# Neighbour lists of a graph network: two tiles sorted in turn, the second sort cut to 32, shorter records

## The reference

```python
def _graph_conv(x, src, dst, W, b, R, num_nodes):
    agg = jax.ops.segment_max(x[src], dst, num_segments=num_nodes)
    agg = jnp.where(jnp.isneginf(agg), 0.0, agg)
    return agg @ W + b + x @ R
...
edge_index = jnp.stack([src, dst])
h = jnp.maximum(_layernorm(x, axis=-1), 0.0)
x = x + _L0_gnn_ref(h, edge_index, ...)
h = jnp.maximum(_layernorm(x, axis=-1), 0.0)
x = x + _L1_gnn_ref(h, edge_index, ...)
```

## Time and profile before

| | us |
|---|---|
| median of three runs | 6179.05 |
| lowest, highest | 6169.71, 6181.23 |
| the profiled execution | 6172.75 |
| its span, first to last instruction | 6170.6 |

### The profile page before, as it was taken

How to read it: one execution, slowest core, us unless ns; L and a number is a source line. 1 busy time by engine, 2 the same in 40 slices (tenths; PEclk the granted TensorE clock), 3 DMA queues, 4 the chain that set the end, 5 groups by cost and what they waited for, 6 DMA issues and landing times. The chain is left out here.

```text
span 6170.6 us, 53373 instructions
## 1 busy us (share of the span) xinstructions
PE 4170.1 (68%) x16801; PEld 1892.4 (31%) x16801; DVE 4641.7 (75%) x7595; ACT 962.0 (16%) x2799; POOL 3126.4 (51%) x3104
## 2 busy tenths in 40 slices
PE   6660001499988881888888677766787587757675
PEld 5430001123322220443444333333333243323332
DVE  7799993477766662999999786767787687768775
ACT  0010000100000001767777300001000100010000
POOL 0300003567777776300000277776777677767776
PEclk9999996799999995999999898888999899979887
DMA  0249921444444441655555443334433443344332
GB/s 16 53 160 420 421 84 42 122 134 128 139 119 120 124 113 41 185 169 162 166 168 176 132 127 105 115 110 114 123 120 115 111 125 115 116 106 122 113 110 70
DMA packets 357598, 819.67 MB, mean 133 GB/s; under 512 B 96893, under 2 KB 211283, under 8 KB 357012
## 3 DMA queue, kind: packets, MB, share of 16 engines
q1 hardware_dynamic: 208468, 564.72, 27.2%
q0 software_dynamic: 99456, 172.85, 11.4%
q10 hardware_dynamic: 49392, 78.70, 4.6%
HBM read 580.78 MB, written 235.22 MB: 132 GB/s over the span
## 5 line engine op out<-in xcount | busy, mean ns | idle before, releaser
L2041 PE MATMUL c_wide<-c_choice,c_parts 128*128 128x512 fp8e4 (+1 forms) x8232 | 1762.8, 371 | 669.0 <-DVE c_even L2129 282.8
L1916 POOL DMA_INDIRECT c_ring<-table,near x1720 | 1652.7, 961 | 524.2 <-issue 524.2
L2041 PEld LDWEIGHTS c_wide<-c_choice,c_parts 128*128 128x128 bf16 x8232 | 809.7, 102 | 1597.6 <-issue 333.9
L2129 DVE TENSOR_TENSOR c_even<-c_even,c_wide 128x896 f32<-128x896 f32 x672 | 726.0, 1080 | 62.9 <-PE c_wide L2041 57.8
L1619 ACT ACTIVATE b_weighed<-b_onehot,mask_r 128x128 f32<-128x128 bf16 x2401 | 719.7, 387 | 228.5 <-DVE b_onehot L1681 228.5
L2129 DVE TENSOR_TENSOR c_odd<-c_odd,c_wide 128x896 f32<-128x896 f32 x644 | 695.8, 1080 | 78.7 <-PE c_wide L2041 74.0
L1658 PE MATMUL b_agg<-b_mass,b_h_row 128*128 128x512 f32 (+1 forms) x1372 | 600.3, 569 | 224.1 <-DVE b_mass L1689 121.3
L2144 DVE TENSOR_REDUCE c_staged<-c_ring 128x128 f32<-128x1024 f32 (+15 forms) x196 | 400.2, 2042 | 419.3 <-DMA c_ring<-table,near 419.1
L1309 PE MATMUL a_logits<-a_hidden,a_w_col 128*49 128x512 f32 (+1 forms) x1372 | 601.6, 562 | 132.6 <-DVE a_hidden L1364 126.2
L1364 DVE TENSOR_TENSOR a_hidden<-a_wide,a_minus_bt 128x896 f32<-128x896 f32 x343 | 373.1, 1088 | 310.9 <-PE a_wide L1290 310.8
L1175 POOL DMA_INDIRECT masks<-a_value,a_cell x430 | 470.2, 1093 | 131.1 <-issue 130.2
(11 more groups left out here) (276 smaller groups left out, 4094.7 us busy)
## 6 DMA issues: line engine op xcount, KB each, us to landing
masks<-n_zeros SPq DMA_DIRECT2D x196, 784.0 KB, 13.7
b_mass<-masks SPq DMA_DIRECT2D x343, 448.0 KB, 3.5
c_choice<-chosen SPq DMA_DIRECT2D x196, 784.0 KB
a_pick_row<-picks ACTq DMA_DIRECT2D x343, 224.0 KB, 3.9
chosen<-a_choice SPq DMA_DIRECT2D x49, 784.0 KB, 4.4
c_ring<-table,near POOLq DMA_INDIRECT x1720
c_source<-table SPq DMA_DIRECT2D x28, 448.0 KB, 6.3
a_ring<-table_a,near POOLq DMA_INDIRECT x430, 3.2
```

Of the source, the lines that this page charges most:

```text
L1916: pool.indirect_dma_start(ring[:, at + j, :], None, table1[layer % 2], bass.IndirectOffsetOnAxis(near[:, u, j:j + 1], 0)).then_inc(landed[ ...
L2041: last = pe.matmul(wide[q][:, lo_c:hi_c], parts[:, s, part, :], choice[e][:, s % CHUNK, lo_c:hi_c], start=(part == 0), stop=(part == 2))
L2129: dve.tensor_tensor(side[:, :], side[:, :], found, ALU.max).then_inc(taken, 1)
```

## The change

The constant `NEAR` is 32. The second sort takes four rounds in place of eight, over the same 64 columns; `record` keeps 32 near neighbours in place of 64, so it has 85 integers, 340 bytes, and `near` and the copies into `laid` are 32 columns shorter. Two tiles are sorted in turn: each step is issued for tile t and tile t+1 after each other, from buffers of their own, and waits for all but the last instruction; the eight instructions of the split become eight such steps. The 49th tile goes alone. The general way is now taken also when a node has more than 32 marked neighbours: `most` becomes the larger of the largest degree and the largest `load` + 32, and is known only behind the sorts, so its spreading by PE and the computation of `slow` and `fast` move there.

```diff
+
+NEAR = 32
...
-RECORD = INFO + BLOCK + TILES
+RECORD = INFO + NEAR + TILES
...
+NEAR_ROUNDS = NEAR // 8
...
-        near = sb("near", [P, TILES, BLOCK], I32)
+        near = sb("near", [P, TILES, NEAR], I32)
...
-            digit_i = sb("n_digit_i", [P, BLOCK], I32)
...
+            work = [[[sb(f"n_work{e}{m}{p}", [P, BLOCK]) for p in range(2)] for m in range(2)] for e in range(2)]
+            top = [[sb(f"n_top{e}{m}", [P, BLOCK]) for m in range(2)] for e in range(2)]
...
             @block.tensor
             def _(pe):
-                pe.wait_ge(most_made, 1)
-                pe.matmul(all_most[:, :], bc(most[:, :], [P, P]), ident[:, :], start=True,
-                          stop=True).then_inc(most_spread, 1)
                 pe.wait_ge(w_loaded, 3 * 16)
                 pe.wait_ge(h_made, 1)
...
                         last.then_inc(ab_made[q], 1)
+                pe.wait_ge(most_made, 1)
+                pe.matmul(all_most[:, :], bc(most[:, :], [P, P]), ident[:, :], start=True,
+                          stop=True).then_inc(most_spread, 1)
 
...
                 own.did(dve.tensor_tensor(degree[:, :], degree[:, :], real[:, :], ALU.mult))
                 own.wait()
                 own.did(dve.tensor_reduce(most[:, :], degree[:, :], AX.X, ALU.max))
-                own.wait()
-                dve.sem_inc(most_made, 1)
-                dve.wait_ge(most_spread, 1)
-                own.did(dve.tensor_reduce(slow[:, :], all_most[:, :], AX.X, ALU.max))
-                own.wait()
-                own.did(dve.tensor_scalar(slow[:, :], slow[:, :], float(BLOCK), None, ALU.is_gt))
-                own.wait()
-                own.did(dve.tensor_scalar(fast[:, :], slow[:, :], -1.0, 1.0, ALU.mult, ALU.add))
 
...
+                def list_begin(t, n, but):
+                    e = t % 2
+                    if n or t >= 2:
+                        listed.wait(but)
+                    if n == 0:
+                        listed.did(dve.tensor_scalar(valid[e][:, :], iota_block[:, :], degree[:, t:t + 1], None,
+                                                     ALU.is_lt))
+                    else:
+                        listed.did(dve.scalar_tensor_tensor(work[e][0][0][:, :], fetched[:, t, :], 1.0, valid[e][:, :],
+                                                            ALU.add, ALU.mult))
+
...
+                def list_split(t, n, but):
+                    e = t % 2
                     listed.wait(but)
                     if n == 0:
-                        listed.did(dve.tensor_scalar(digit_i[:, :], top[0][:, :], -1.0, None, ALU.add))
+                        listed.did(dve.tensor_scalar(digit_i[e][:, :], top[e][0][:, :], -1.0, None, ALU.add))
...
                     elif n == 1:
-                        listed.did(dve.tensor_scalar(masked_i[:, :], digit_i[:, :], P - 1, None,
+                        listed.did(dve.tensor_scalar(masked_i[e][:, :], digit_i[e][:, :], P - 1, None,
                                                      ALU.bitwise_and))
...
-                        listed.did(dve.tensor_scalar(digit_i[:, :], digit_i[:, :], 7, None,
+                    elif n == 2:
+                        listed.did(dve.tensor_scalar(digit_i[e][:, :], digit_i[e][:, :], 7, None,
                                                      ALU.arith_shift_right))
-                    elif n == 2:
-                        listed.did(dve.tensor_scalar(lo_of[:, t, :], masked_i[:, :], 1.0, None, ALU.add))
-                        listed.did(dve.tensor_copy(hi_of[:, t, :], digit_i[:, :]))
-                        listed.did(dve.tensor_tensor(again[:, 1:BLOCK], digit_i[:, 1:BLOCK],
-                                                     digit_i[:, 0:BLOCK - 1], ALU.is_equal))
                     elif n == 3:
-
-                        listed.did(dve.tensor_tensor(work[1][0][:, :], again[:, :], top[0][:, :], ALU.mult))
+                        listed.did(dve.tensor_tensor(again[e][:, 1:BLOCK], digit_i[e][:, 1:BLOCK],
+                                                     digit_i[e][:, 0:BLOCK - 1], ALU.is_equal))
+                    elif n == 4:
...
+                        listed.did(dve.tensor_scalar(lo_of[:, t, :], masked_i[e][:, :], 1.0, None, ALU.add))
+                    elif n == 6:
+                        listed.did(dve.tensor_copy(hi_of[:, t, :], digit_i[e][:, :]))
                     else:
-                        listed.did(dve.tensor_scalar(counted[:, :], work[1][0][:, :], 0.0, 0.0, ALU.is_gt,
+                        listed.did(dve.tensor_scalar(counted[e][:, :], work[e][1][0][:, :], 0.0, 0.0, ALU.is_gt,
                                                      ALU.add, accum_out=load[:, t:t + 1]))
...
-                def list_step(t, n, ahead):
-                    r, but = n // 2, int(ahead)
-                    if n % 2 == 0:
-                        find(1, r, but)
-                        if ahead and n == 0:
-                            list_begin(t + 1)
-                        elif ahead:
-                            remove(0, r - 1, but)
+                def list_end(t, n, but):
+                    e = t % 2
+                    listed.wait(but)
+                    if n == 0:
+                        listed.did(dve.tensor_scalar(empty[e][:, :], top[e][1][:, 0:NEAR], 0.0, float(ZERO_ROW + 1),
+                                                     ALU.is_equal, ALU.mult))
                     else:
+                        listed.did(dve.scalar_tensor_tensor(record[:, t, INFO:INFO + NEAR], top[e][1][:, 0:NEAR],
+                                                            -1.0, empty[e][:, :], ALU.add, ALU.add))
+
+                own.wait()
+                dve.wait_ge(block_fetched, TILES * 16)
+                for pair in range(0, TILES, 2):
+                    both = range(pair, min(pair + 2, TILES))
+                    but = len(both) - 1
+                    for n in range(2):
+                        for t in both:
+                            list_begin(t, n, but)
+                    for r in range(ROUNDS):
+                        for t in both:
+                            find(t % 2, 0, r, but)
                         if r < ROUNDS - 1:
-                            remove(1, r, but)
-                        else:
-
-                            listed.wait(but)
-                            listed.did(dve.tensor_scalar(empty[:, :], top[1][:, :], 0.0,
-                                                         float(ZERO_ROW + 1), ALU.is_equal, ALU.mult))
-                        if ahead:
-                            find(0, r, but)
-
-                own.wait()
-                dve.wait_ge(block_fetched, TILES * 16)
-                list_begin(0)
-                for r in range(ROUNDS):
-                    find(0, r, 0)
-                    if r < ROUNDS - 1:
-                        remove(0, r, 0)
-                for n in range(5):
-                    list_split(0, n)
-                for t in range(TILES):
-                    ahead = t < TILES - 1
-                    for n in range(2 * ROUNDS):
-                        list_step(t, n, ahead)
-                    list_end(t, int(ahead))
-                    if ahead:
-                        for n in range(5):
-                            list_split(t + 1, n, but=int(n == 0))
+                            for t in both:
+                                remove(t % 2, 0, r, but)
+                    for n in range(8):
+                        for t in both:
+                            list_split(t, n, but)
+                    for r in range(NEAR_ROUNDS):
+                        for t in both:
+                            find(t % 2, 1, r, but)
+                        if r < NEAR_ROUNDS - 1:
+                            for t in both:
+                                remove(t % 2, 1, r, but)
+                    for n in range(2):
+                        for t in both:
+                            list_end(t, n, but)
+                listed.wait()
+                own.did(dve.tensor_reduce(most_load[:, :], load[:, :], AX.X, ALU.max))
+                own.wait()
+                own.did(dve.tensor_scalar(most_load[:, :], most_load[:, :], float(BLOCK - NEAR), None, ALU.add))
+                own.wait()
+                own.did(dve.tensor_tensor(most[:, :], most[:, :], most_load[:, :], ALU.max))
+                own.wait()
+                dve.sem_inc(most_made, 1)
                 for s in range(TILES):
...
 
-                picks_of = record[:, :, INFO + BLOCK:RECORD]
+                dve.wait_ge(most_spread, 1)
+                own.did(dve.tensor_reduce(slow[:, :], all_most[:, :], AX.X, ALU.max))
+                own.wait()
+                own.did(dve.tensor_scalar(slow[:, :], slow[:, :], float(BLOCK), None, ALU.is_gt))
+                own.wait()
+                own.did(dve.tensor_scalar(fast[:, :], slow[:, :], -1.0, 1.0, ALU.mult, ALU.add))
+                own.wait()
+                picks_of = record[:, :, INFO + NEAR:RECORD]
```

(66 more changed lines are left out.)

3 lines of the change are left out of this document (1 added, 2 removed).

## The result

The changed kernel takes 6079.88 us in the median of four runs (6077.1 to 6085.81), the kernel before 6177.09 in four (6169.71 to 6181.23). The ratio is 0.9844, 95% interval 0.9832 to 0.9856: 97 us faster.

What follows compares the result with a forecast made beforehand. VectorE's work in the neighbour lists and the search of the picks was taken to bound the front stage. -96.1 + 1.6 - 2.4 - 1.2 = -98.1 us gave 6074.7 profiled, with 6.3 added a median of 6081; range 6062 to 6108.

Steps and rivals of the forecast that it cites:

- What is last: End of the lists and search stage: VectorE still ends it, at about 840, the clearing of `masks` 25 us earlier.
- The pair: Neighbour lists: two tiles sorted in step take 9.90 us; the lists take 246.9 us in place of 343.0, 96.1 saved.
- The moved reductions: Behind the sorts and the search: seven dependent steps at 0.23 us add 1.6 us, all on the path.
- The records: Load back of shorter records: 2.4 us saved, the middle between 4.7 if bytes set the time and nothing if runs do.
- The copies into `laid`: 49 copies, each 32 columns shorter: 49 x 0.025 = 1.2 us saved, between 0 and 2.
- The base: Whole kernel: profiled execution 6172.75 us becomes 6074.7; the median, 6.3 above the profiled one, becomes 6081.
- The attribution: Neighbour lists: four rounds dropped from the second sort save 64 us with both tiles in step, the shadowed splits the rest.
- The coarser cadence: Rival, neighbour lists: 10.5 to 11 us a pair, lists save 72 to 82 us, median 6093 to 6106; chance 0.19.
- the absence of overlap: Rival, neighbour lists: VectorE doesn't overlap the two tiles, 16.1 us a pair, 6228 us in all; chance 0.02.
- a loss in later stages: Rival, stages from 1125.1 us on: something there gives back 20 to 40 us; chance 0.10.
- The general way: Rival: the new limit sends the whole graph to gathers in groups of four, over 12000 us; chance 0.01.

Runs made afterwards that it cites:

- e4: The changed kernel searching the picks of only 24 of 49 source tiles, writing 0 for the others; 6045.72 us, 34 below the changed kernel.
- e7: The changed kernel with lists of 56 columns in place of 64; ratio 0.9806 to the kernel before at 7723.37 us.
- e6: The changed kernel with each record loaded back as one run, seven transfers in place of 21; load back 11.7 us in place of 18.8.
- e2: The kernel before with only the second sort cut to four rounds and records of 85 integers; 6160.62 us, ratio 0.9971.
- e3: The changed kernel with each step of a pair waiting for all instructions before it, not all but the last; 6285.22 us.
- e8: The changed kernel with the limit for the general way at 24 marked neighbours in place of 32; 36220.43 us.
- e11: The changed kernel as it is, run once more on a slower chip; 7673.82 us, ratio 0.9847 to the kernel before at 7786.74.

## Why the prediction was right

6081 was predicted and 6079.88 measured. Step by step:

- **What is last.** VectorE ends the stage, and the clearing has ended 32.0 us ahead of it; 25 was predicted. Of the 7 us between, 3.0 are VectorE's smaller gain and 3.6 the clearing's own earlier end, which the prediction had standing still. e4 and e7 show the second limit acting.
- **The pair.** 10.03 us against 9.90. The sorts were priced right to a hundredth (4.81, and 2.22 for 2.21) from the double round. Of the steps that no row of before showed, the split took 1.96 for 1.92 and the start 0.60 for 0.53: two instructions `n_valid` stand 0.16 us apart, more than the 0.11 that was taken for all. The lists saved 92.2 with the 0.7 of the first reductions in it, 92.9 for the 96.1 predicted; this is the only term with an error above 1 us.
- **The moved reductions.** +0.74 ahead of the search and +0.70 behind it (840.16 to 840.86), 1.6 predicted.
- **The records.** 2.2 us against 2.4. The middle between "bytes" and "runs" was a choice and not a working, and that it came so near is luck. The 17 us in it stand in no row that it names: they are the time that SP's issues of the load back take from first to last. With the runs and the transfers unchanged, the 27% fewer bytes gave these 2.2 us; a third of the runs and of the transfers gave 7.1 (e6). Which of those two it is stays open.
- **The copies into `laid`.** 0.4 us against 1.2. A copy is 0.014 us shorter (medians of 0.192 and 0.178), not 0.025.
- **The base.** The sum gives 6074.7 for a profiled execution and it took 6077.1. The 6.3 us added for the median were a difference among three runs, and the median above the profiled execution turned out 2.8 this time; that the median came within 1 us is partly luck, as is that the 2.4 us missing in the sum and this offset cancelled.
- **The attribution.** The text ahead of the result gave 64 us to the dropped rounds "with both tiles in step", and that condition carries it: e2 shows 10 us for them without it.
- **The rivals.** The coarser cadence (10.5 or more), the absence of overlap and a loss in later stages didn't come. The first was priced 1 to 2 us too low: 0.6 and 1.1 us more in 24 pairs make 6095 and 6107, not 6093 and 6106. The absence of overlap was priced at 16.1 us a pair from durations; e3, which takes the overlap away, shows 18.6, since the gaps between dependent steps come on top. The general way doesn't act on these data; its price was named at over 12000 us, and e8 shows 36220 on the slower chip: the sum had GpSimd's gathers alone, without what GpSimd stands between groups and without the attention stage.

Left open: what makes the later stages a quarter slower on two of the four chips. In e11 the stretch behind the first gather takes 1615 us more than in the changed kernel's first profile. VectorE is busy in it as long as there (3779 and 3776 us), GpSimd a little less (2973 and 3021), and TensorE 250 us more (4078 and 3828). So most of the difference is time in which the engines stand, and the lower granted clock accounts for 250 us of it at most as far as TensorE's own work goes. What they stand for wasn't tried.

## What to carry to other kernels

A chain of small dependent VectorE instructions is bound by how long a step waits for the one before it. Here a second independent chain in step cost hardly more than one alone (0.65 us a round of both, 0.58 a round of one), and a third chain brought next to nothing (4.85 us a tile in place of 5.02). Before rounds are taken out of a loop, look at what they share their time with: the cut was worth 10 us where its partner stayed behind and 66 where both chains shrank together. And read the wait of the engine that is not last at a barrier: it is about the most that speeding up the last one can bring. It is no fixed number: the clearing here ended up to 7 us earlier or later from one kernel to the next, and some 11 us later on two of the chips.

## What the runs showed of the hardware

- VectorE, instructions of 64 columns: 0.11 to 0.16 us from start to start when the next doesn't wait for the one before (0.20 for a MATCH_REPLACE8 with its MATCH_VALUE_LOAD), 0.23 to 0.27 when it does, as in the lone last tile; a double round of MAX8 and MATCH_REPLACE8 0.65 against 1.16 us (e3).
- Loading 6272 records of 340 bytes took 11.7 us as one run each in seven transfers, and 18.8 as three runs of 16, 128 and 196 bytes in 21 transfers (e6). As three of 16, 256 and 196 bytes in 21 transfers it took 21.0 (the kernel before).
- One and the same kernel took 6178, 6175, 7723 and 7787 us on four chips, at a granted clock of 0.90 on the first two and 0.81 to 0.82 on the others. The lists, search and ranks agree within a few us among them (the first gather of `table_b` in the changed kernel at 1031.6 and 1034.2), while the stretch behind it, which gathers single rows from DRAM, takes 5043 us in one case (6074.9 - 1031.6) and 6658 in the other (7692.4 - 1034.2).
